# A four-layer graph attention kernel: the loop over pairs of groups written out in straight code

## The chip, the cores and the metric

The kernel runs on one core of a Trainium2 chip. The metric is the device time of one execution in microseconds (us). The profile is a record of one such execution by the hardware profiler.

## The reference

Four graph attention layers follow each other on 8192 nodes with 128 features, over one 8192 x 8192 adjacency matrix of 0 and 1. Cut to what matters:

```python
h = jnp.maximum(_layernorm(x, axis=-1), 0.0)      # before each layer
Wh = h @ W                                        # 8192 x 128
e = leaky_relu((Wh @ a1)[:, None] + (Wh @ a2)[None, :], 0.2)
attention = softmax(where(adj > 0, e, very_negative), axis=1)
x = x + act(attention @ Wh)                       # act: none in layer 0, elu in 1 to 3
# layer 2 also drops attention below 1e-4, multiplies by the row's number of neighbours
# and adds its own Wh ahead of the elu
```

## The kernel before, in words

The output rows are cut into 16 groups of 512 (`GROUPS`). For one group in one layer (a sweep), the kernel goes over 64 tiles of 128 neighbours. For each tile VectorE (DVE) makes a 128 x 512 tile of unnormalised attention, `q`, from a row, a column and a mask of bits (L632), and TensorE (PE) multiplies it by `vals` into `acc` with 4 matmuls of 128 x 129 (L862). These are f32, and the profile shows each as two MATMUL and two LDWEIGHTS records, so one tile is 8 records of each kind and one group 512. `q` is a ring of 8 tiles (`RING`): DVE can be 8 tiles ahead of PE and no more. Every 16 tiles (a chunk) DVE first unpacks a mask from bits with 8 instructions (L604).

While a group is summed, the group before it is finished: ScalarE (ACT) and DVE scale its sums, add the residual and normalise the rows, PE turns them (L781) and multiplies them by the next layer's weights (L789; layers 0 to 2 only). In layer 0 the adjacency matrix is also read for the first time: SyncE (SP) queues its pieces, ACT makes them binary, and PE packs them into bits (L814). Layer 2 has 64 extra small matmuls a chunk that count neighbours (L869), and one extra pass over a single group behind it (the "redo" pass).

Each engine has its own instruction stream, and they meet at semaphores only. All four layer-long walks over the 16 groups on SP, DVE, PE and ACT go through `every_group`: group 0 in straight code, then a hardware loop of 7 iterations over two groups each (groups 1 and 2, 3 and 4, ..., 13 and 14), then group 15 in straight code. At the end of each iteration stand L85's `REGISTER_ALU` and `COMPARE_AND_BRANCH`: it jumps back 6 times in a layer, behind groups 2, 4, ..., 12, and falls through once. That makes 24 jumps back in four layers on each of the four engines.

Two other loops stand in the kernel: `every_quad` (L95), which reads the first rows ahead of layer 0, and the redo loop.

Of the kernel before, what the change touches and what calls it, by code (L numbers as in the profile page):

```python
# [22 lines left out]
GROUPS = N // W  # L23
# [57 lines left out]
def every_group(eng, body, tail):  # L81

    body(Group(0, 0), None, True)
    with eng.Fori(0, GROUPS // 2 - 1) as p:  # L85
        body(Group(p, 1), Group(p, 0), True)
        body(Group(p + 1, 0), Group(p, 1), True)
    body(Group(GROUPS // 2 - 1, 1), Group(GROUPS // 2 - 1, 0), False)
    tail(Group(GROUPS // 2 - 1, 1))
# [38 lines left out]
def build(nc, x, adj, ws, avs, out):  # L128
# [12 lines left out]
    with ExitStack() as ctx:  # L141
# [150 lines left out]
        def _(sp):  # L292
# [41 lines left out]
            for k in range(4):  # L334
# [18 lines left out]
                if k == 0:  # L353

                    def transfers(g, before, more):
                        for i in range(PIECES):
                            if more and i == 12:
                                if before is None:
                                    store_rows(k)
                                load_row(k, after(g))  # L360
                            if before and i == 22:
                                store(before)
                            if before and i == 27:
                                load_after(before)
                            if more:
                                to = after(g)
                                load_piece(to.value * PIECES + i, i % ADJ_RING, to.value, i)

                    every_group(sp, transfers, store)
                    for b in range(2):  # L370
                        sp.wait_ge(x_out[k][b], 16 * (GROUPS // 2))
                    continue

                def transfers_of_rows(g, before, more):
# [4 lines left out]
                    if before:  # L379
                        store(before)  # L380
                        load_after(before)

                every_group(sp, transfers_of_rows, store)
                for b in range(2):
                    sp.wait_ge(x_out[k][b], 16 * (GROUPS // 2))
# [40 lines left out]
        def _(dve):  # L426
# [336 lines left out]
            for sw in MAIN:  # L763
                start_of_layer(sw)
                every_group(dve, body(sw), last_tail(sw))
                if sw == 2:
                    thresholds()
                    with dve.Fori(0, dve.value_load(redo_groups[0:1, 0:1], min_val=1, max_val=GROUPS)) as p:
                        g = RedoGroup(p)
                        body(REDO)(g, None, False)  # L770
                        last_tail(REDO)(g)
                        dve.wait_ge(wh_ready[REPROJECT], g.value + 1)
# [347 lines left out]
```

## Time and profile before

| what | before |
|---|---|
| median of 3 runs | 4456.36 us (4451.89 to 4457.23) |
| the profiled execution's own time | 4454.27 us |
| its span in the profile | 4452.1 us |
| PE busy | 4185.0 us |
| DVE busy | 3722.2 us |
| ACT busy | 1060.9 us |
| granted TensorE clock, mean | 0.966 |

The span runs from the first to the last instruction of the program; the time of the execution is 2.2 us longer. Busy times are sums over instructions that work; register, branch and semaphore instructions are not in them. The granted clock is a share of the full TensorE clock.

### The profile page before, as it was taken

To read this page: it belongs to the slowest core of one execution; us is meant where nothing else is said; L and a number is where in the kernel's file an instruction comes from. 1 tells how busy PE (TensorE), PEld (TensorE's weight loads), DVE (VectorE), ACT (ScalarE), POOL (GpSimd) and SP (SyncE) were. 2 spreads that over 40 slices of the span, in tenths; PEclk is the share of its full clock that TensorE was granted. 3 is DMA by queue.
4 is the path that set the end of the run, shared out by engine and by line. 5 is a ranking of instruction groups with operands and counts; after the bars stand their busy time and mean duration, and the time that the engine had idled before them with its cause. 6 is when DMAs were issued, how large, how long until landed. Compare 5 with 4: busy or idle time off the path is not lost.

```text
span 4452.1 us, 107788 instructions
## 1 busy us (share of the span) xinstructions
PE 4185.0 (94%) x42322; PEld 4148.2 (93%) x42322; DVE 3722.2 (84%) x8069; ACT 1060.9 (24%) x1639; POOL 6.6 (0%) x31
## 2 busy tenths in 40 slices
PE   4999999999989999999989999999996899999999
PEld 4899999999989999999989999999995799999999
DVE  5777777877889999999888888878878889988888
ACT  4566666666411111111110111111110100000000
POOL 0000000000000000000000000000000000000000
PEclk8899999999989999999989999999998899999999
DMA  6787787878400000000010000000000000000000
GB/s 191 226 264 244 245 252 245 263 245 251 154 11 16 16 14 16 16 14 14 13 46 16 14 11 14 16 11 14 14 9 8 11 16 16 14 15 16 12 15 13
DMA packets 367405, 335.19 MB, mean 75 GB/s; under 512 B 12800, under 2 KB 359168, under 8 KB 366848
## 3 DMA queue, kind: packets, MB, share of 16 engines
q1 hardware_dynamic: 366848, 327.34, 23.6%
q8 instruction: 401, 6.57, 0.6%
q14 instruction: 156, 1.28, 0.1%
HBM read 305.93 MB, written 21.36 MB: 74 GB/s over the span
## 4 chain that ended last, share of the span: by engine, by line
PE 85%; issue 7%; DVE 5%; ACT 2%; DVEq 0%; DMA 0%; POOL 0%; ACTq 0%; POOLq 0%; SPq 0%
PE acc L862 79%; DVE q L632 3%; PE acc L869 2%; PE ps_pack L814 2%; PE ps_wh L789 1%; DVE mask L604 1%; PE ps_wh L781 1%; ACT e L942 1%; DVE t L525 0%; ACT adj_bf L965 0%; ACT L935 0%; PE ps_bc L838 0%; ACT hT L948 0%; DVEq L631 0%; ACT wh L954 0%
## 5 line engine op out<-in xcount | busy, mean ns | idle before, releaser
L862 PE MATMUL acc<-vals,q 128*128 128x129 f32 x33280 | 3925.6, 279 | 116.1 <-DVE q L632 62.1
L862 PEld LDWEIGHTS acc<-vals,q 128*128 128x128 f32 x33280 | 3819.4, 194 | 131.3 <-issue 68.6
L632 DVE SCALAR_TENSOR_TENSOR q<-rrow,R,mask 128x512 f32<-128x512 f32 x4160 | 2958.5, 749 | 372.9 <-PE acc L862 176.5
L965 ACT ACTIVATE adj_bf<-adj_int,threshold 128x1024 bf16<-128x1024 int32 x480 | 545.5, 1147 | 285.4 <-PE ps_pack L814 279.6
L604 DVE TENSOR_SCALAR mask<-bits 128x512 uint16 (+1 forms) x2080 | 443.4, 289 | 94.7 <-issue 56.4
L1020 ACT ACTIVATE xnew<-acc,rec 128x128 f32<-128x128 f32 x192 | 54.6, 367 | 936.0 <-DVE rec L658 936.0
L814 PEld LDWEIGHTS ps_pack<-packer,adj_bf 128*128 128x128 bf16 x4096 | 177.4, 97 | 10.6 <-ACT adj_bf L965 2.0
L814 PE MATMUL ps_pack<-packer,adj_bf 128*128 128x32 bf16 x4096 | 181.0, 177 | 1.3 <-DVE adj_bf L506 0.6
L942 ACT ACTIVATE e<-xnew,nm,rs 128x128 f32<-128x128 f32 x228 | 93.8, 483 | 246.5 <-DVE nm L471 246.5
L948 ACT ACTIVATE hT<-ps_wh 128x512 f32<-128x512 f32 x65 | 38.8, 597 | 448.9 <-PE ps_wh L781 448.9
L781 PE MATMUL ps_wh<-ident,e 128*128 128x128 f32 x260 | 48.9, 320 | 82.1 <-ACT e L942 82.1
L781 PEld LDWEIGHTS ps_wh<-ident,e 128*128 128x128 f32 x260 | 34.2, 162 | 87.2 <-ACT e L942 82.4
L869 PEld LDWEIGHTS acc<-validb,mask 128*128 128x128 fp8e4 x4096 | 111.9, 95 | 0.8
L935 ACT ACTIVATE sd<-ve 128x4 f32<-128x4 f32 x65 | 13.2, 203 | 413.0 <-DVE ve L451 412.9
L869 PE MATMUL acc<-validb,mask 128*128 128x1 bf16 x4096 | 111.5, 163 | 0.0
L954 ACT ACTIVATE wh<-ps_wh 128x512 f32 (+1 forms) x65 | 38.8, 597 | 299.4 <-PE ps_wh L789 299.2
L677 DVE SCALAR_TENSOR_TENSOR xnew<-mean,none,xnew 128x128 f32<-128x128 f32 x192 | 66.0, 347 | 47.8 <-ACT xnew L1020 47.8
L1027 ACT ACTIVATE e<-xnew 128x512 f32<-128x512 f32 x49 | 30.9, 631 | 308.4 <-DVE xnew L677 244.4
L789 PE MATMUL ps_wh<-w_sb,hT 128*128 128x130 f32 x520 | 91.6, 331 | 8.7 <-ACT hT L948 8.7
L458 DVE RECIPROCAL rs<-sd 128x4 f32<-128x4 f32 x65 | 11.5, 176 | 103.4 <-ACT sd L935 103.4
L789 PEld LDWEIGHTS ps_wh<-w_sb,hT 128*128 128x128 f32 x520 | 79.6, 233 | 11.8 <-ACT hT L948 11.8
L432 DVE BATCH_NORM_STATS2 stats<-xnew 128x6 f32<-128x128 f32 x228 | 62.5, 287 | 2.1 <-DMA xnew<-in_x_dram 2.0
(101 smaller groups left out, 698.8 us busy)
## 6 DMA issues: line engine op xcount, KB each, us to landing
adj_int<-in_adj_dram SPq DMA_DIRECT2D x512, 512.0 KB, 4.7
rrow<-rows_of_layers SPq DMA_DIRECT2D x60, 256.0 KB, 3.1
xin<-x_between_layers SPq DMA_DIRECT2D x33, 256.0 KB, 2.8
x_between_layers<-xnew SPq DMA_DIRECT2D x32, 256.0 KB, 2.3
xin<-in_x_dram SPq DMA_DIRECT2D x24, 256.0 KB, 5.0
x_of_layer<-xnew SPq DMA_DIRECT2D x17, 256.0 KB, 2.3
wh_of_layer<-wh SPq DMA_DIRECT2D x1, 4096.0 KB, 15.9
xin<-x_of_layer SPq DMA_DIRECT2D x16, 256.0 KB, 2.8
```

The source lines that it names most:

```text
L432: last = nc.vector.bn_stats(stats[:, b, :], xt[:, b, :])
L604: last = nc.vector.tensor_scalar(mask_words[:, buf, :, b, :], bits[:, g.value, c * JC:(c + 1) * JC, :], amount, ONES, op, ALU.bitwise_and)
L632: nc.vector.scalar_tensor_tensor(q[:, j % RING, :], rrow[:, g.parity, :], column(R, c * JC + j), mask[:, buf, j, :], ALU.max, ALU.mult).th ...
L677: last = nc.vector.scalar_tensor_tensor(o[:, b, :], mean[:, :], none4[:, b:b + 1], o[:, b, :], ALU.mult, ALU.add)
L781: last = nc.tensor.transpose(ps_tr[:, b * P:(b + 1) * P], h[:, b, :], ident[:, :])
L789: last = nc.tensor.matmul(projected[:, b // 2, b % 2, :], hT[:, b, :], w_sb[:, layer_of(k), :], start=True, stop=True)
L814: last = nc.tensor.matmul(ps_pack[:, at:at + WORDS], adj_bf[:, slot, b, t * P:(t + 1) * P], packer[:, b, :], start=(b == 0), stop=(b == BL ...
L862: last = nc.tensor.matmul(a[:, b // 2, at:at + F + 1], q[:, j % RING, b * P:(b + 1) * P], vals[:, t, :], start=(t == 0 and b % 2 == 0), st ...
L869: last = nc.tensor.matmul(a[:, 0, at:at + 1], mask_fp8[:, c % 2, n, b * P:(b + 1) * P], validb[:, c * JC + n:c * JC + n + 1], start=False, ...
L942: last = nc.scalar.activation(h[:, b, :], xt[:, b, :], ACT.Relu, bias=nm[:, b:b + 1], scale=rs[:, b:b + 1])
L965: nc.scalar.activation(adj_bf[:, to, :, :], adj_int[:, slot, :, :], ACT.Sigmoid, scale=STEEP, bias=threshold[:, 0:1]).then_inc(adj_binary, 1)
L1020: last = nc.scalar.activation(o[:, b, :], acc[g.parity][:, b // 2, at:at + F], ACT.Copy, scale=scale)
```

## The change

One line changes: the hardware loop in `every_group` becomes a Python loop, which writes its body out 7 times when the program is built. The group's number is then a constant everywhere in it.

```diff
     body(Group(0, 0), None, True)
-    with eng.Fori(0, GROUPS // 2 - 1) as p:
+    for p in range(GROUPS // 2 - 1):
         body(Group(p, 1), Group(p, 0), True)
         body(Group(p + 1, 0), Group(p, 1), True)
     body(Group(GROUPS // 2 - 1, 1), Group(GROUPS // 2 - 1, 0), False)
```

The program of PE grows from 7314 to 25534 entries (an f32 matmul is one entry here), that of DVE from 3345 to 8628, of ACT from 733 to 2141, of SP from 428 to 774. What is computed, and in which order, is the same on each engine.

PE in layer 3 before, from the straight group 0 into the loop body and out of it (`acc`, `vals`, `q` as above; L845 turns a row; L85 ISA sets up the loop's register):

```order
L862 MATMUL acc<-vals,q 128x129 x32
L845 MATMUL ps_bc<-ident,r 64x128
L862 MATMUL acc<-vals,q 128x129 x224
L85 UNCONDITIONAL_BRANCH
L85 ISA
L858 ISA
L862 MATMUL acc<-vals,q 128x129 x4
L858 REGISTER_ALU
...
L85 REGISTER_ALU
L85 COMPARE_AND_BRANCH
L862 MATMUL acc<-vals,q 128x129 x256
L141 UNCONDITIONAL_BRANCH
```

The same place in PE's stream after the change:

```order
L850 MATMUL ps_wh<-w_sb,h_mean 128x128
L838 MATMUL ps_bc<-diag,ones 128x128 x4
L862 MATMUL acc<-vals,q 128x129 x32
L845 MATMUL ps_bc<-ident,r 64x128
L862 MATMUL acc<-vals,q 128x129 x4064
L141 UNCONDITIONAL_BRANCH
```

The matmuls of all 16 groups now stand in one row (32 + 4064 = 16 x 256), with no jump and none of the register instructions (one for each of 127 tiles of the pair, and the set-up) between them.

DVE in layer 3 before, at the end of the loop body and the start of the straight group 15 (the last `q` of a group, then the masks of the next):

```order
L632 SCALAR_TENSOR_TENSOR q<-rrow,R,mask 128x512
L631 REGISTER_ALU
L632 SCALAR_TENSOR_TENSOR q<-rrow,R,mask 128x512
L85 REGISTER_ALU
L85 COMPARE_AND_BRANCH
L604 TENSOR_SCALAR mask<-bits 128x16x32 x8
L632 SCALAR_TENSOR_TENSOR q<-rrow,R,mask 128x512 x11
L647 COPY den<-acc 128x4
```

The same place in DVE's stream after the change:

```order
L632 SCALAR_TENSOR_TENSOR q<-rrow,R,mask 128x512 x16
L604 TENSOR_SCALAR mask<-bits 128x16x32 x8
L632 SCALAR_TENSOR_TENSOR q<-rrow,R,mask 128x512 x11
L647 COPY den<-acc 128x4
L632 SCALAR_TENSOR_TENSOR q<-rrow,R,mask 128x512
```

The order of the work is the one of before; the branch and the register instructions between the `q` tiles are gone.

## Rows read from the trace of the kernel before

**Rows 1.** The page's head and part 1: busy us, share of the span, instructions.

```profile
span 4452.1 us, 107788 instructions
PE 4185.0 (94%) x42322; PEld 4148.2 (93%) x42322; DVE 3722.2 (84%) x8069; ACT 1060.9 (24%) x1639; POOL 6.6 (0%) x31
```

**Rows 2.** Busy time by stretch: groups 2 to 13 of layers 0, 1, 2, 3.

```profile
core 0: us, PE busy (x) PEld busy (x) DVE busy (x) ACT busy (x) POOL busy (x), PEclk, DMA share, GB/s
267.66:1116.58 848.92, 826.12 (x9363) 818.87 (x9362) 652.98 (x1452) 538.33 (x613) 0.00 (x0) 0.98 0.80 250
1383.44:2099.49 716.05, 705.36 (x6290) 704.23 (x6289) 659.92 (x1465) 98.27 (x204) 0.00 (x0) 1.00 0.05 15
2382.98:3202.77 819.79, 798.59 (x9363) 796.86 (x9362) 671.72 (x1453) 98.24 (x204) 0.00 (x0) 0.98 0.05 14
3600.09:4328.59 728.50, 700.40 (x6146) 698.78 (x6145) 646.92 (x1273) 28.88 (x72) 0.00 (x0) 0.98 0.05 15
```

**Rows 3.** Waits of PE, layer 3, window 3600 to 4328.6.

```profile
PE acc L862 <- issue: 14.2, 6, 2.7
PE acc L862 <- DVE q L632: 13.9, 6, 2.5
```

**Rows 4.** PE's timeline in layer 3, window 3640 to 3800.

```profile
3659.88 0.60 PE L862 MATMUL acc<-vals,q 128*128 128x129 f32 x3 [2.33 <-DVE q L632]
3662.93 115.52 PE L862 MATMUL acc<-vals,q 128*128 128x129 f32 x1021 [2.46 <-issue]
3780.74 0.60 PE L862 MATMUL acc<-vals,q 128*128 128x129 f32 x3 [2.29 <-DVE q L632]
```

**Rows 5.** Timeline of all engines, window 3648 to 3672: the DVE rows.

```profile
3653.72 1.71 DVE L604 TENSOR_SCALAR mask<-bits 128x512 uint16 x8 [2.54 <-issue]
3655.57 5.39 DVE L632 SCALAR_TENSOR_TENSOR q<-rrow,R,mask 128x512 f32<-128x512 f32 x8
```

**Rows 6.** Instructions of L85: ns min/median/max.

```profile
L85 DVEq COMPARE_BRANCH  x28: 55/63/78, 326.1 to 4379.0; - x28
L85 PEldq COMPARE_BRANCH  x28: 76/4116/5019, 334.3 to 4384.0; - x28
```

**Rows 7.** Busy time by stretch, one group each, columns as in rows 2.

```profile
200.05:267.66 67.61, 67.61 (x788) 67.19 (x784) 55.35 (x122) 44.37 (x50) 0.00 (x0) 1.00 0.84 266
1116.58:1184.44 67.86, 67.76 (x782) 67.17 (x781) 54.60 (x121) 44.91 (x52) 0.00 (x0) 1.00 0.72 230
2040.99:2099.49 58.50, 58.50 (x523) 58.50 (x524) 55.34 (x123) 6.82 (x15) 0.00 (x0) 1.00 0.05 15
2099.49:2158.01 58.52, 58.52 (x527) 58.52 (x526) 55.12 (x123) 8.19 (x17) 0.00 (x0) 1.00 0.04 11
3202.77:3268.02 65.25, 65.25 (x783) 65.20 (x782) 56.11 (x122) 8.19 (x17) 0.00 (x0) 1.00 0.04 10
3542.91:3600.09 57.18, 57.18 (x514) 57.18 (x513) 54.42 (x109) 2.41 (x6) 0.00 (x0) 1.00 0.05 15
3659.87:3721.00 61.13, 58.67 (x512) 58.59 (x512) 53.89 (x107) 2.41 (x6) 0.00 (x0) 0.97 0.05 14
4328.59:4385.77 57.18, 57.18 (x514) 57.18 (x513) 53.97 (x107) 2.41 (x6) 0.00 (x0) 1.00 0.04 11
```

**Rows 8.** PE's timeline, window 4255 to 4450, its last row.

```profile
4270.53 172.69 PE L862 MATMUL acc<-vals,q 128*128 128x129 f32 x1533 [2.18 <-issue]
```

**Rows 9.** Timeline, window 4322 to 4334: DVE's tiles for layer 3's group 14.

```profile
4324.26 8.07 DVE L632 SCALAR_TENSOR_TENSOR q<-rrow,R,mask 128x512 f32<-128x512 f32 x11
```

**Rows 10.** The page's part 3: packets, MB, share of 16 engines.

```profile
q8 instruction: 401, 6.57, 0.6%
q14 instruction: 156, 1.28, 0.1%
```

**Rows 11.** DMA in the gapless layer 3 group 1, window 3542 to 3600.

```profile
q8 instruction: 4, 0.07, 0.5%
```

## The prediction

> **What bounds the kernel now.** I read four things in this order: the busy times, the busy times by stretch, the timeline of PE around the places where the loop jumps back, and the instructions of line 85.
>
> The page says that PE works 4185.0 of 4452.1 us [rows 1]. So PE is the bound, and the question is what it does in the other 6%. I cut layers into groups at the first weight load of each group and looked at the stretch from group 2 to group 13 in every layer, since these twelve groups hold all six jumps back. PE's idle time there is the stretch less its busy time [rows 2]: 848.92 - 826.12 = 22.8 us in layer 0, 716.05 - 705.36 = 10.7 in layer 1, 819.79 - 798.59 = 21.2 in layer 2, 728.50 - 700.40 = 28.1 in layer 3. Together that is 82.8 us.
>
> In layer 3 this idle time has just twelve pieces, six put down to "issue" and six to DVE's `q` [rows 3]. The timeline shows where: at a jump back PE stops for 2.33 us, does 3 matmuls, and stops again for 2.46 us. Then it runs 1021 matmuls, a pair of groups, without a stop, to the next jump back [rows 4]. So the loss is bound to the jump, not to the work.
>
> The label "DVE q" must not be taken at its word. DVE had begun the eight tiles of the new group at 3655.57, and a tile takes some 0.75 us, so the first was ready near 3656.3 [rows 5]. PE started on it at 3659.88 [rows 4], some 3.5 us later. The instructions of line 85 name the real cause: PE's COMPARE_BRANCH takes 4.1 us in the median of 28, and 0.076 us at the least [rows 6]. There are 24 that jump and 4 that fall through, so the long ones are those that jump. During that time PE's queue runs empty. DVE's branch itself is short (63 ns), but behind it DVE's next instruction comes 2.54 us later [rows 5, 6], so it pays for the jump too, hidden in the eight tiles that it is ahead.
>
> The jump costs more than the idle time. Layer 3's group 3, which follows a jump, takes 61.13 us at a granted clock of 0.97, with the second stop in it. Groups 1 and 14, with no jump ahead of them, take 57.18 at 1.00 [rows 7]. Of those 3.95 us only some 2.5 are the stop [rows 4]. The rest is the clock: a mean of 0.97 says that, behind the two stops, a part of the group ran at the lower of the two levels, 1.2 instead of 2.4 GHz.
>
> **The change, part by part.** It removes the 24 jumps on each of four engines. For the price I put each stretch of twelve groups beside twelve groups of the same layer that no jump touches, since that takes in the stops and the low clock together.
>
> - Layer 0: group 1 takes 67.61 and group 14 takes 67.86 us [rows 7]. Six of each are 812.8. The stretch took 848.92 [rows 2]: 36.1 us to win.
> - Layer 1: groups 13 and 14 take 58.50 and 58.52 [rows 7]. 716.05 - 6 x 117.02 = 13.9 us.
> - Layer 2: group 14 takes 65.25. 819.79 - 12 x 65.25 = 36.8 us.
> - Layer 3: groups 1 and 14 take 57.18. 728.50 - 12 x 57.18 = 42.3 us.
>
> The sum is 129.1 us: 82.8 of idle time and 46.3 of low clock and its like.
>
> It also removes the register instructions, one for each tile on PE and DVE. I cost that at nothing. Layer 3's last three groups run in one row, 1533 matmuls in 172.69 us with no stop [rows 8], and two of them are in the loop with registers while the last is straight with constants. Group 15, the straight one, starts at 4385.77 [rows 7] and ends with that row at 4443.22, which is 57.45 us with the tail of its last matmul in it; group 14, in the loop, takes 57.18. The cover is the matmuls themselves. If a register instruction were uncovered, its going would be a gain, and the two groups leave no more than some 0.1 us a group for that, 5 us over 48 groups.
>
> What could DVE do once PE no longer waits? The stops give DVE time to refill its ring, and that goes away. But at the start of layer 3's group 14, where nothing has jumped, DVE begins its tiles at 4324.26 [rows 9] and PE comes to them at 4328.59 [rows 7]. The first was ready some 3.6 us ahead. Its work per group is 53.97 us of 57.18 [rows 7], so it keeps up with a PE that never stops. In layer 0 and 2 it has 54.60 of 67.86 and 56.11 of 65.25. The tightest is layer 1 with 55.34 of 58.50. I cost DVE at nothing; without that margin, one us late in each of 48 groups would cost 48 us.
>
> SP and ACT lose their jumps too. In layer 0 the DMA moves 250 GB/s over the stretch and 266 in group 1 without a jump [rows 2, 7]. The same bytes in 812.8 us need 250 x 848.92 / 812.8 = 261 GB/s, just under what group 1 shows. If DMA could not go over 250, layer 0 would give back its 36.1 us.
>
> The longer program adds instruction fetch, if anything. The trace shows 401 blocks of 16 KB on queue 8 (6.57 MB) [rows 10]. PE's matmuls and weight loads alone are 2 x 42322 [rows 1]. Both code queues moved 7.85 MB [rows 10] for 107788 instructions [rows 1], 73 bytes each with what was read and not used, so I estimate 64 bytes an instruction and PE's share at 331 blocks. So PE already reads its code as it goes, in the loop as well. Group 1 of layer 3 took in 4 blocks while it ran at full speed without a stop [rows 7, 11]. The straight code reads the same way, so I cost this at nothing. The blocks that are read anew at jumps go away.
>
> The profiled execution took 4454.27 us; less 129.1 that is 4325.2. The median of the runs is 2.1 us above it, so I predict a median of 4327 us.
>
> **The rivals.**
>
> 1. The jump itself is cheap and the stops stay, because something else makes them (the first `q` of a pair, a semaphore). If a branch is worth the 0.076 us of the shortest one [rows 6], 24 of them are worth 1.8 us, and the time is 4456.4 - 1.8 = 4455. For it speaks the label "DVE q" on half of the stops [rows 3]. Against it: group boundaries inside the pair have the same work and no stop [rows 4, 8]. The Trainium skill has a rule on this side: its page "Advanced Engine Details and Errata", section "Control Flow Timing", gives about 108 ns for a compare-and-branch. By that figure the 24 would be worth 2.6 us, and no difference could be measured; the trace agrees for the branches that fall through, not for those that jump.
> 2. The idle time goes but the low clock stays, because it comes from something periodic. Then 4456.4 - 82.8 = 4374. Against it: groups 1 and 14 show 1.00 [rows 7].
> 3. DMA bounds layer 0. Then 4327 + 36 = 4363. Against it: the 266 GB/s of group 1. For it: DMA is 0.84 busy there, and one group is not twelve.
> 4. Slower: reading straight code is not hidden. Each block of 16 KB would bring PE a stop. From 129.1 / 331 = 0.39 us a block on, the change loses; at the 2.5 us that a stop behind a jump takes, it would be 331 x 2.5 = 828 us, thus 5155. For it speaks that a wait for code is what the jump shows, and that the program is 3.5 times as long. Against it: 1533 matmuls, some 12 blocks of code, ran with no stop [rows 8]. The same skill, page "Runtime: NRT & Kernel Launch", section "Instruction fetch mechanics", says that sequential reading is mostly hidden, and that branches break it; that row agrees.
>
> **How the numbers follow.** My forecast gets 0.86, rival 1 gets 0.03, rival 2 gets 0.03, rival 3 gets 0.05, rival 4 gets 0.03. The forecast's own range is 4314 to 4342: down by the 5 us of register instructions and by as much again for the first groups of the layers, up by a tenth of the sum for groups that are disturbed by something else, as layers show here and there. For the range I take 4312 to 4346, a little wider at both ends, which leaves out the rivals, 0.14 in all. A measurement of this kernel tells 0.2%, 9 us, from no change. Faster by more than that: forecast and rivals 2 and 3, 0.94. The same: rival 1, 0.03. Slower: rival 4, 0.03.
>
> **What the profile after would show.** PE's timeline in layer 3 has rows of thousands of matmuls with no "idle before" between groups 2 and 13. The stretches of twelve groups take 813, 702, 783 and 686 us. All 12 groups of a layer are at a clock of 1.00. Line 85 has no row. Queue 8 moves some 335 to 345 blocks in place of 401. PE's busy time falls by some 46 us, although it does the same matmuls. I would be wrong if the groups show short stops at even distances (rival 4), if layer 0 has waits of ACT for `adj_int` (rival 3), or if groups alternate as before (rivals 1 and 2).

## The result and the profile after

The changed kernel takes 4326.71 us in the median of 4 runs (4325.96 to 4328.15), the kernel before 4455.47 us beside it. The ratio is 0.9712, with a 95% interval from 0.9696 to 0.9729. The forecast was 4327 us. All ratios here leave out two executions that took far longer than the others of their kernels, 15516 us (once, with 105 added instructions) and 5445 us (once, the kernel before); I have no explanation for them.

The profiled execution of the changed kernel has a span of 4324.1 us, 128.0 less than before. Its head, busy times and code queues on the page, the lines that answer to [rows 1] and [rows 10]:

```profile
span 4324.1 us, 96787 instructions
PE 4138.4 (96%) x42322; PEld 4106.4 (95%) x42322; DVE 3730.6 (86%) x8069; ACT 1056.1 (24%) x1637; POOL 6.5 (0%) x31
...
q8 instruction: 330, 5.41, 0.5%
q14 instruction: 90, 0.74, 0.1%
```

PE does the same 42322 matmuls in 46.6 us less busy time. Queue 8 reads 71 fewer blocks of code.

The stretches of groups 2 to 13 of layers 0 to 3, as in [rows 2] (span, then busy us and count of each engine, granted clock, DMA share, GB/s):

```profile
core 0: us, PE busy (x) PEld busy (x) DVE busy (x) ACT busy (x) POOL busy (x), PEclk, DMA share, GB/s
267.15:1081.31 814.16, 813.01 (x9363) 806.35 (x9362) 654.05 (x1452) 536.46 (x612) 0.00 (x0) 1.00 0.83 261
1348.45:2050.61 702.16, 702.16 (x6291) 702.16 (x6290) 662.67 (x1465) 98.23 (x204) 0.00 (x0) 1.00 0.05 15
2334.35:3117.37 783.02, 783.02 (x9363) 782.42 (x9362) 673.26 (x1453) 98.17 (x204) 0.00 (x0) 1.00 0.05 14
3514.46:4200.62 686.16, 686.16 (x6147) 686.16 (x6146) 648.79 (x1273) 28.82 (x72) 0.00 (x0) 1.00 0.05 15
```

The forecast for them was 813, 702, 783 and 686 us. They sum to 2985.50 us, against 848.92 + 716.05 + 819.79 + 728.50 = 3113.26 before, so 127.8 of the 128.0 us come from these stretches. PE's busy time equals the stretch in three of them, and the clock is 1.00 in all four; before, it was 0.98 in three.

PE's timeline from the start of layer 3's group 1 to the end of the layer, which answers to [rows 4] and [rows 8], is a single row with no idle time in it:

```profile
3459.73 855.52 PE L862 MATMUL acc<-vals,q 128*128 128x129 f32 x7659
```

DVE keeps its lead. In the timeline around the start of layer 3's group 7, it goes to the new group's tiles right behind the masks, as in [rows 9]:

```profile
3794.19 1.70 DVE L604 TENSOR_SCALAR mask<-bits 128x512 uint16<-128x512 uint16 x8
3794.30 0.33 SPq L304 DMA_DIRECT2D rrow<-rows_of_layers  x1
3795.93 7.28 DVE L632 SCALAR_TENSOR_TENSOR q<-rrow,R,mask 128x512 f32<-128x512 f32 x10
```

### The profile page after: what moved, and what is told of

Read it like the earlier page. It is cut to its first block, busy times and chain, and to the rows that moved or that the text cites. A ratio compares the mean times of both kernels' runs of the same rounds, so it can differ in the third digit from the quotient of the medians.

```text
span 4324.1 us, 96787 instructions
## 1 busy us (share of the span) xinstructions
PE 4138.4 (96%) x42322; PEld 4106.4 (95%) x42322; DVE 3730.6 (86%) x8069; ACT 1056.1 (24%) x1637; POOL 6.5 (0%) x31
## 4 chain that ended last, share of the span: by engine, by line
PE 94%; issue 4%; ACT 2%; DVE 1%; POOL 0%; ACTq 0%; POOLq 0%; DVEq 0%
PE acc L862 86%; PE acc L869 2%; PE ps_pack L814 2%; PE ps_wh L789 2%; PE ps_wh L781 1%; ACT e L942 1%; ACT hT L948 0%; DVE t L525 0%; PE ps_bc L838 0%; ACT wh L954 0%; ACT diag L995 0%; ACT xnew L1020 0%; POOL packer L414 0%; DVE xnew L677 0%; DVE q L632 0%
## 5 line engine op out<-in xcount | busy, mean ns | idle before, releaser
L862 PE MATMUL acc<-vals,q 128*128 128x129 f32 x33280 | 3881.8, 277 | 34.0 <-DVE q L632 34.0
L862 PEld LDWEIGHTS acc<-vals,q 128*128 128x128 f32 x33280 | 3779.2, 192 | 44.7 <-DVE q L632 28.4
L604 DVE TENSOR_SCALAR mask<-bits 128x512 uint16<-128x512 uint16 (+1 forms) x2080 | 442.7, 288 | 19.1 <-ACT taurow L1002 10.4
L954 ACT ACTIVATE wh<-ps_wh 128x512 f32<-128x512 f32 (+1 forms) x65 | 38.8, 597 | 299.8 <-PE ps_wh L789 299.8
L458 DVE RECIPROCAL rs<-sd 128x4 f32<-128x4 f32 x65 | 11.4, 175 | 104.7 <-ACT sd L935 104.7
L1020 ACT ACTIVATE xnew<-acc,kappa 128x128 f32<-128x128 f32 x68 | 19.4, 369 | 249.3 <-DVE kappa L668 155.7
```

The costliest lines, as they stand in the source:

```text
L604: last = nc.vector.tensor_scalar(mask_words[:, buf, :, b, :], bits[:, g.value, c * JC:(c + 1) * JC, :], amount, ONES, op, ALU.bitwise_and)
L862: last = nc.tensor.matmul(a[:, b // 2, at:at + F + 1], q[:, j % RING, b * P:(b + 1) * P], vals[:, t, :], start=(t == 0 and b % 2 == 0), st ...
L1020: last = nc.scalar.activation(o[:, b, :], acc[g.parity][:, b // 2, at:at + F], ACT.Copy, scale=scale)
```

## The experiments

**Which engine's jump costs.** Two kernels part PE from the rest. In the first only PE's walk is straight:

```diff
-def every_group(eng, body, tail):
+def every_group(eng, body, tail, straight=False):
+    def pair(p):
...
+    for p in range(GROUPS // 2 - 1 if straight else 0):
+        pair(p)
+    if not straight:
+        with eng.Fori(0, GROUPS // 2 - 1) as p:
+            pair(p)
...
-                every_group(pe, body(sw), last_tail(sw))
+                every_group(pe, body(sw), last_tail(sw), True)
```

> Only PE's walk over the groups is straight code; SP, DVE and ACT keep the hardware loop. My theory (PE's own jump makes the stops, and DVE's 2.5 us behind its jump is hidden in the eight tiles that it is ahead): the time is that of the changed kernel, 4327 us, within 5 us. The rival (DVE's late q makes the stops that carry its name, in layers 1 and 3, 24.6 us of idle time by the waits plus the low clock behind them): about 4327 + 40 = 4367 us.

It took 4328.06 us, a ratio to the kernel before of 0.9712 (0.9695 to 0.9728), the same as that of the full change. Its timeline shows DVE's jump where it was, between layer 3's groups 2 and 3, and PE running through it (every line of this kernel is 3 further down; L89 is the loop, L607 the masks, L635 `q`, L865 the matmuls):

```profile
3569.80 20.38 PE L865 MATMUL acc<-vals,q 128*128 128x129 f32 x181
3569.91 20.18 PEld L865 LDWEIGHTS acc<-vals,q 128*128 128x128 f32 x180
3570.18 1.71 DVE L607 TENSOR_SCALAR mask<-bits 128x512 uint16 x8 [2.44 <-issue]
3572.03 7.38 DVE L635 SCALAR_TENSOR_TENSOR q<-rrow,R,mask 128x512 f32<-128x512 f32 x11
```

DVE stands for 2.44 us behind its branch; PE has no "idle before" (time in square brackets, in which the engine stood idle ahead of the row). The second kernel is the mirror image: `straight=True` as the default and `False` for PE, so that PE alone keeps the hardware loop.

> SP, DVE and ACT are straight, PE alone keeps the hardware loop. My theory: nothing is won, 4455 us within 5 us, and PE's 24 long branches and its stops stand as before. The rival (DVE's late q makes half of the stops): some 40 us faster, 4415 us.

It took 4451.70 us, ratio 0.9992 (0.9982 to 1.0002): nothing that can be told from no change. PE's stops in layer 3 stand as in [rows 4], and now the trace puts all of them down to "issue":

```profile
3656.61 0.59 PE L865 MATMUL acc<-vals,q 128*128 128x129 f32 x3 [2.67 <-issue]
3659.66 117.05 PE L865 MATMUL acc<-vals,q 128*128 128x129 f32 x1021 [2.46 <-issue]
3779.33 0.60 PE L865 MATMUL acc<-vals,q 128*128 128x129 f32 x3 [2.62 <-issue]
```

So the label "DVE q" was a coincidence in time. Queue 8 counts 401 blocks in this kernel and 330 in the one with PE alone straight: it is PE's code queue.

The DMA records of the kernel before show what PE waits for. At the jump of [rows 4], PE's branch starts at 3655.49 and takes 4.13 us. A block of PE's code is read from 3657.00 to 3658.12, and the branch ends 1.5 us behind that. The next block is read from 3660.27 to 3661.40, and PE's second stop ends at 3662.93, again 1.5 us behind it. The queue's rows for the windows 3656.9 to 3660.2 and 3660.2 to 3662.9 have just these two:

```profile
q8 instruction: 1, 0.02, 2.1%
q8 instruction: 1, 0.02, 2.6%
```

It is the same at all 24 jumps: PE's branch ends 1.3 to 2.3 us behind the end of such a read, and each of the six second stops of layer 3 ends 1.3 to 1.5 us behind the end of the next one. The 48 blocks that are read in groups 2 to 13 of layer 3 after the change are followed by no stop. So I read both stops as waits for code. A control comes at the end of this section: a jump back with no block read beside it.

**Half of the jumps.** The first three pairs straight, the last four a loop, on all engines:

```diff
-    with eng.Fori(0, GROUPS // 2 - 1) as p:
+    for p in range(3):
+        body(Group(p, 1), Group(p, 0), True)
+        body(Group(p + 1, 0), Group(p, 1), True)
+    with eng.Fori(3, GROUPS // 2 - 1) as p:
```

> The first three pairs of each layer are straight, the last four a loop, on all engines: 12 jumps back in place of 24. If every jump costs its own stops and low clock, half of the 129 us comes back: 4326.7 + 64.5 = 4391 us, within 5 us. If the loss were one of a longer program or of the loop as such (entering it, its register instructions), it would be near 4455 or 4327.

It took 4383.24 us, ratio 0.9834 (0.9817 to 0.9850): 72.7 us less than the 4455.98 of the kernel before beside it, where half of the gain would be 64.4, and 8 us below the time that I expected. Most of the loss goes with the number of jumps, but not all jumps cost the same. PE's timeline in layer 3 shows it:

```profile
3966.28 2.27 PE L865 MATMUL acc<-vals,q 128*128 128x129 f32 x18 [1.80 <-DVE q L635]
3969.61 112.51 PE L865 MATMUL acc<-vals,q 128*128 128x129 f32 x1006 [1.06 <-issue]
```

The body and its work are the same as in [rows 4]. But the second stop comes behind 18 matmuls, not 3, and lasts 1.06 us, not 2.46. In layer 0 it is the other way round: three waits of PE there come to 15.2 us, over 5 us a jump, where [rows 2] gave 22.8 us for six (window 260 to 1180):

```profile
PE acc L865 <- issue: 15.2, 3, 5.6
```

So the 8 us are what is left of differences in both directions. What has changed for the body is where in memory it begins; the next two kernels test that alone.

**The place of the jump's target.** The kernel before, with 105 or 211 instructions more at the start of PE's program (the builder puts two waits into one instruction); the second kernel has 422 for 210:

```diff
             pe.wait_ge(weights_in, 16 * 12)
+            for _ in range(210):
+                pe.wait_ge(weights_in, 16 * 12)
             pe.wait_ge(consts_ready, CONSTS)
```

> The kernel before, with 105 more instructions in PE's program, all at its very start (waits that are already met), so that each loop body begins 105 instructions later in memory. If the size of a stop depends on where the jump's target lies in the 16 KB blocks in which code is read, the second stop of layer 3 (2.2 to 2.7 us, 6 times) goes or moves, and the stops of other layers change; the kernel gains some 10 to 20 us less up to 5 us for the added waits. If the second stop belongs to layer 3's work, it stays where it is, and the time is 4456 to 4461 us.

It took 4431.12 us in the median of 4 runs, ratio 0.9946 (0.9926 to 0.9966). The kernel is 25 us faster for having more instructions. In PE's timeline of layer 3 (L864 are the matmuls here) the second stop is gone:

```profile
3654.79 1.95 PE L864 MATMUL acc<-vals,q 128*128 128x129 f32 x16
3658.29 114.62 PE L864 MATMUL acc<-vals,q 128*128 128x129 f32 x1024 [1.56 <-DVE q L632]
3775.01 5.17 PE L864 MATMUL acc<-vals,q 128*128 128x129 f32 x44 [2.10 <-DVE q L632]
```

In layer 1, which had one stop a jump before, there is now a second at four of the six jumps, behind 16 matmuls:

```profile
1443.18 2.05 PE L864 MATMUL acc<-vals,q 128*128 128x129 f32 x16 [1.52 <-DVE q L632]
1446.39 3.84 PE L864 MATMUL acc<-vals,q 128*128 128x129 f32 x32 [1.16 <-DVE q L632]
```

Its stretches of groups 2 to 13 against those of [rows 2]: 28.2 us less in layer 3, 7.3 less in layer 2, 4.1 less in layer 0, 7.5 more in layer 1. That is 32.2 in all; some 3.8 us go to the added waits, by which layer 0's stretch begins later (271.43, not 267.66). That leaves 28.4, against 29.0 between the two profiled executions (4425.22 and 4454.27).

```profile
271.43:1116.21 844.78, 824.01 (x9362) 816.76 (x9361) 652.90 (x1452) 538.03 (x613) 0.00 (x0) 0.99 0.80 252
1382.88:2106.39 723.51, 708.22 (x6290) 706.03 (x6289) 659.88 (x1465) 98.21 (x204) 0.00 (x0) 1.00 0.05 15
2389.46:3201.94 812.48, 797.97 (x9362) 796.24 (x9361) 671.66 (x1453) 98.17 (x204) 0.00 (x0) 0.98 0.05 14
3599.28:4299.58 700.30, 689.37 (x6147) 688.25 (x6146) 646.12 (x1273) 28.83 (x72) 0.00 (x0) 1.00 0.05 15
```

> The same with 211 instructions, up to 11 us of added waits at the start. If the place in the block decides, the stops differ again from those of the kernel before and of the shift by 105, and one layer may get a second stop that it did not have; if not, each layer has its stops as before.

It took 4451.17 us, ratio 0.9990 (0.9980 to 1.0000). Its stops differ again: layer 0 is the one that pays now, with 861.70 us in its stretch in place of 848.92, and PE's waits in layer 0 (window 260 to 1150) are

```profile
PE acc L864 <- issue: 35.6, 6, 8.1
```

that is 5.9 us a jump, one of them 8.1, where [rows 2] gave 22.8 us for six. That the whole kernel takes as long as the one before is chance: its layer 0 begins 16.7 us later (284.37, not 267.66) behind the added waits, which I had put at 11 us at most, and its four stretches take 20.1 us less (3093.18 against 3113.26). Layer 3's stretch is 699.76 us, as with the shift by 105, and layer 1's is 718.26. The same loop thus costs layer 3 between 13.6 us (699.76 - 686.16) and 42.3 us by its place alone. The block reads say in what way the place counts. In layer 3 with the shift by 105, the read behind the branch ends at 3659.95, while PE is at work on the 1024 matmuls, and no stop follows; before the shift PE had 3 matmuls to do until then, and stood. In layer 0 with the shift by 211 it has none: the first branch ends at 354.53, and PE goes on at 358.08, behind the next block. So a second stop is short, long or absent by how much work PE finds between the jump's target and the next block. I worked out positions in blocks of 256 instructions from the program, but could not make all the second stops fit one rule, so which place is a bad one can't be told from the program as far as these runs go.

**The cover of DVE's jump.** A ring of 4 `q` tiles in place of 8 takes half of DVE's lead away. First all straight:

```diff
-RING = 8
+RING = 4
```

> The changed kernel (all straight) with a ring of 4 q tiles in place of 8: DVE can be only 3.6 us ahead of PE. It is the ground for the next run. Slower than 4327 us, since the smallest lead in layer 0 was 0.8 us and in layers 1 and 3 some 3 us with eight tiles: some 2.7 us in each of 15 groups of layer 0 and below 1 us in chunks of layers 1 and 3, about 4430 us, between 4380 and 4500.

It took 4365.83 us, ratio 0.9801 (0.9785 to 0.9817). That is 39 us more than with eight tiles, not the 100 that I expected: in layer 0, where I had put 2.7 us into each group, the trace shows no stop of PE over 0.4 us past group 0. PE's waits for `q` over the whole run are 59.8 us in place of 34.0, and its busy time for the same matmuls is 4152.0 us in place of 4138.4; these two, 25.8 and 13.6 us, make up the 39. I had added up leads as if a late tile could not be made up; that was wrong, and which part of the reckoning fails stays open. Then the same ring with PE alone straight:

> Ring of 4 again, PE straight, but SP, DVE and ACT with the hardware loop. My theory (DVE's jump costs nothing only because eight tiles cover it): with four tiles its 2.1 to 2.5 us, and in layer 0 some 3.7, behind the masks' 1.8 us show up in PE's idle time at most of the 24 jumps, 40 to 70 us more than the run with ring 4 and all straight. The rival (DVE's jump is harmless as such): the same time as that run.

It took 4428.12 us, ratio 0.9941 (0.9924 to 0.9957), 62.3 us more than the run before. With eight tiles the same two kernels stood at 4328.06 and 4326.71. PE's waits for `q` are 96.9 us here, 37.1 more, and its busy time is 4175.7 us, 23.7 more; no other wait of PE grew by more than 1.3 us, so SP's and ACT's jumps play no part that shows. The timeline at a jump in layer 1:

```profile
1444.77 1.71 DVE L607 TENSOR_SCALAR mask<-bits 128x512 uint16 x8 [2.38 <-issue]
...
1446.62 8.18 DVE L635 SCALAR_TENSOR_TENSOR q<-rrow,R,mask 128x512 f32<-128x512 f32 x11
...
1447.51 7.72 PE L865 MATMUL acc<-vals,q 128*128 128x129 f32 x67 [1.44 <-DVE q L635]
```

Here the label is right: `q` begins at 1446.62, its first tile takes some 0.75 us, and PE starts at 1447.51.

These stops lower PE's clock too, though PE itself does not jump. Behind the one in layer 3 that ends at 3764.27, and behind the second stop of [rows 4] in the kernel before, PE runs at the lower level for a while (columns as in [rows 2], clock 0.50):

```profile
3765.20:3768.60 3.40, 3.40 (x18) 3.40 (x18) 2.33 (x4) 0.00 (x0) 0.00 (x0) 0.50 0.02 5
3662.93:3665.70 2.77, 2.77 (x14) 2.77 (x14) 0.75 (x1) 0.00 (x0) 0.00 (x0) 0.50 0.00 0
```

**The other loop.** The changed kernel with `every_quad` straight too:

```diff
-    with eng.Fori(1, CHUNKS - 1) as m:
+    for m in range(1, CHUNKS - 1):
```

> The changed kernel with the other loop (every_quad, line 95, two iterations of four groups each, ahead of layer 0) written out as well. PE's branch there takes 0.25 us and no stop follows it, since its body and target are near each other in memory. A group of rows takes PE 6.46 us in that loop and 6.27 outside it, so 8 x 0.19 = 1.5 us could be won: 4325 us, which cannot be told from 4327. If every loop back cost what it does in every_group, it would be 2 x 5 = 10 us faster, 4317.

It took 4325.64 us in the median of 5 runs, ratio 0.9703 (0.9689 to 0.9716). That is 1.1 us below the changed kernel, which fits the first expectation and not the 4317 us of the second, and is not to be told from no difference. This loop is the control for what a jump costs by itself: in the kernel with the shift by 105 PE's branch there goes back at 73.81 and takes 0.24 us, and no block of PE's code is read between 61.5 and 110.6. A jump back alone is thus cheap, and what makes it 4.1 us in `every_group` is the wait for a block that has to be read.

## Why the prediction was right, point by point

- **PE's own branch makes the stops, not DVE's `q`.** Shown: PE alone straight gives the whole gain, all but PE straight gives none. That it waits there for its code is read from the block reads at all 24 jumps and from the 0.24 us of a jump with none; no run was built to take the reads away and leave the jumps.
- **The sum of 129.1 us.** The four terms were 36.1, 13.9, 36.8 and 42.3 us. By the stretches they measured 34.8, 13.9, 36.8 and 42.3. Layer 0's is 1.3 too large, because I took its group 1 (67.61 us) for half of the groups. It comes behind group 0 and is 0.25 us shorter than the others; with group 14 alone the term would have been 34.6. That the forecast hit to 0.3 us is in part luck: the profiled execution took 4326.30 us, 1.1 more than the 4325.2 of the sum, and the median of the runs lies 0.4 above it, not 2.1.
- **46 us of low clock beside 83 us of idle time.** PE's busy time fell by 46.6 us for the same matmuls, and all stretches show 1.00. That stops lower the clock is shown by the ring of 4 with PE alone straight, where stops of another origin are followed by a clock of 0.50. But not every stop does: in layer 3 of the shift by 211 PE's waits at the jumps come to 11.4 us, yet the clock is 1.00 and PE's busy time 688.35 us, 2.2 above the 686.16 of the changed kernel. The forecast did not need to tell them apart, since it priced both together.
- **Register instructions at nothing.** Layer 3's groups take 686.16 / 12 = 57.18 us with constants, as groups 1 and 14 took with registers. Right, and the 5 us that I had left for them were not there.
- **DVE at nothing.** Right at a ring of 8. The runs with a ring of 4 show that the ring is the cover: with half of it DVE's jumps cost 62 us.
- **DMA in layer 0.** It moves 261 GB/s over the whole stretch, as worked out, so rival 3 fell.
- **Code reading at nothing.** 330 blocks, a little under the 335 to 345 that I named and next to the 331 estimated for matmuls and weight loads. They came with no stop in PE's last 855 us, so rival 4 fell. The Trainium skill, page "Runtime: NRT & Kernel Launch", section "Instruction fetch mechanics", has it the same way: it says that reading code in sequence is mostly hidden, and that a taken branch to code not yet at hand stalls until that is read. The trace agrees on both, with no stop in those 855 us and the waits for blocks behind the 24 jumps. The Trainium skill, page "Advanced Engine Details and Errata", section "Control Flow Timing", gives some 108 ns for a compare-and-branch, by which (an estimate) the 24 would be worth 2.6 us. The measurement decides: with their stops and the clock, 24 jumps of PE cost 128 us, 5.3 us each.
- **The range.** Its working does not give its ends: 5 us twice below 4327 is 4317, not 4314, and a tenth of the sum above it is 4340, not 4342. The result lies far inside either.
- **What the prediction lacked.** It took a jump's price as a property of the layer. It is one of the layer and of the place in memory, as the shifts show; the sum came out to the microsecond since it priced the jumps of this very program by its own trace. The same sum for the shift by 105 would be 95.6 us (3081.07 - 2985.50), and for the shift by 211 107.7.

## What to carry to other kernels

A hardware loop need not be free on the engine that bounds the kernel (here 5.3 us a jump back): look at the time just behind its jump back, and price a loop by comparing iterations that a jump precedes with iterations that none precedes. Write out that engine's walk, and leave the loop on engines that are some microseconds ahead of it, as long as a buffer covers their jump. Do not trust the releaser that a wait is put down to when its tile was ready long before the wait ended, and beware of small edits to a looping program: they move its code, and that alone moved this one by 0.5%. Where a stop follows a jump, look whether a block of the engine's code lands just ahead of its end.

## What the runs showed that I had not expected

More instructions made the kernel faster: 105 of them at the start of PE's program took 25 us off it, in layer 3 alone 28.2 us, and gave layer 1 a second stop of 1.16 us at jumps where it had none. With 211 the stops of layer 0 grew from some 3.8 to 5.9 us a jump. And a ring of half the size cost only 39 us, or 0.9%, as long as the walk over the groups had no jump.
